# A softmax shift broadcast by two wide matmuls on a table written ahead, in place of four narrow ones

## The reference, cut to what matters

```
h = (x @ W).reshape(N, H, C)
al_s = jnp.einsum('nhc,hc->nh', h, a_src)
al_d = jnp.einsum('nhc,hc->nh', h, a_dst)
e = jax.nn.leaky_relu(al_s[src] + al_d[dst], 0.2)
m = jax.ops.segment_max(e, dst, num_segments=N)
ex = jnp.exp(e - m[dst])
denom = jax.ops.segment_sum(ex, dst, num_segments=N)
alpha = ex / (denom[dst] + 1e-16)
out = jax.ops.segment_sum(h[src] * alpha[:, :, None], dst, num_segments=N)
```

## Time and profile before

| | |
|---|---|
| median of 3 runs | 1179.64 us (1179.39 to 1180.54) |
| the profiled execution's own time | 1182.3 us, of which the span of the trace is 1180.2 us |
| PE busy | 1115.9 us, 95% of the span |
| DVE busy | 839.0 us, 71% |
| ACT busy | 513.9 us, 44% |
| POOL busy | 54.3 us, 5% |
| mean granted clock of TensorE | 0.984 of full speed |

### The profile page before, as it was taken

The page is one execution under the profiler, slowest core; times in us unless marked ns, Lnnn a source line. Parts: engine busy times, 40 slices in busy tenths (PEclk is TensorE's granted clock), DMA queues, the critical chain, the costliest instruction groups (busy, mean ns, idle before and its releaser), DMA issues. The chain is left out here.

```text
span 1180.2 us, 17595 instructions
## 1 busy us (share of the span) xinstructions
PE 1115.9 (95%) x7126; PEld 1045.3 (89%) x7126; DVE 839.0 (71%) x1394; ACT 513.9 (44%) x1052; POOL 54.3 (5%) x50
## 2 busy tenths in 40 slices
PE   5999999999999999999999999858999899999998
PEld 5878886789989998999999999758999899899998
DVE  7998896889768887789668778879757633341163
ACT  4232322376447654556547644335536612431110
POOL 4200001020000000000000000520000000000000
PEclk9999999989999999999999999968999999999999
DMA  6133130021011100201020100022002200000321
GB/s 230 68 103 117 41 122 18 1 63 54 1 42 49 54 1 1 90 22 34 1 68 23 54 1 1 10 91 72 27 27 103 83 1 1 27 14 1 131 77 55
DMA packets 27618, 58.44 MB, mean 50 GB/s; under 512 B 3492, under 2 KB 6152, under 8 KB 27536
## 3 DMA queue, kind: packets, MB, share of 16 engines
q1 hardware_dynamic: 27344, 56.96, 14.5%
q10 hardware_dynamic: 192, 0.32, 0.1%
HBM read 41.73 MB, written 15.54 MB: 49 GB/s over the span
## 5 line engine op out<-in xcount | busy, mean ns | idle before, releaser
L1456 PE MATMUL banks<-hs,ring_hi 128*128 128x258 f32 (+1 forms) x1600 | 299.8, 288 | 6.8 <-DVE z L1051 6.8
L1456 PEld LDWEIGHTS banks<-hs,ring_hi 128*128 128x128 f32 (+1 forms) x1600 | 249.0, 188 | 8.7 <-DVE z L1051 8.0
L1456 PE MATMUL banks<-hs,ring_lo 128*128 128x258 f32 (+1 forms) x800 | 227.1, 284 | 0.0
L247 ACT ACTIVATE e<-banks,al 128x256 f32<-128x256 f32 (+1 forms) x500 | 194.6, 493 | 38.0 <-PE banks L232 38.0
L1456 PEld LDWEIGHTS banks<-hs,ring_lo 128*128 128x128 f32 (+1 forms) x800 | 150.8, 189 | 0.0
L255 ACT ACTIVATE ring_hi<-pf 128x512 fp32r<-128x512 f32 (+1 forms) x125 | 81.6, 652 | 134.7 <-DVE pf L266 130.1
L1486 PE MATMUL banks<-w_hi,oT_hi 128*128 128x384 f32 (+1 forms) x320 | 109.5, 342 | 5.9 <-DVE shiftT L1130 4.5
L1486 PE MATMUL banks<-w_lo,oT_hi 128*128 128x384 f32 (+1 forms) x320 | 108.3, 338 | 0.0
L1486 PE MATMUL banks<-w_hi,oT_lo 128*128 128x384 f32 (+1 forms) x320 | 108.2, 338 | 0.0
L264 DVE TENSOR_TENSOR e<-e 128x512 f32<-128x512 f32 (+1 forms) x125 | 84.5, 676 | 33.2 <-ACT e L247 32.7
L1330 PE MATMUL banks<-w_hi,xT_hi 128*128 128x512 f32 x240 | 96.7, 403 | 1.2 <-DVE xT_lo L827 0.6
(11 more groups left out here) (265 smaller groups left out, 2106.2 us busy)
## 6 DMA issues: line engine op xcount, KB each, us to landing
h_scratch<-stage SPq DMA_DIRECT2D x30, 256.0 KB, 2.0
hs<-h_scratch SPq DMA_DIRECT2D x30, 256.0 KB, 2.9
w_st<-in_L_gnn_W SPq DMA_DIRECT2D x4, 1536.0 KB, 7.4
w_st<-in_L_gnn_W SPq DMA_DIRECT2D x16, 384.0 KB, 3.4
gw_st<-in_L_gnn_W SPq DMA_DIRECT2D x12, 384.0 KB, 4.2
xr<-in_x SPq DMA_DIRECT2D x9, 384.0 KB, 10.1
rows<-in_x SPq DMA_DIRECT2D x9, 384.0 KB, 5.8
x_scratch<-rows SPq DMA_DIRECT2D x9, 384.0 KB
```

What stands on the lines that cost most here:

```text
L247: last = nc.scalar.activation(self.e[:, local % 2, a, i, 0:n], self.p_shift[:, a, 0:n], ACT.Exp, bias=scores[a][:, g * G + i:g * G + i + 1])
L1456: last = nc.tensor.matmul(p_a[0:m, dt, half, 0:HH], wt.ring[a][:, s // G, s % G, dt * P:dt * P + m], hs[:, s, b, half * HH:(half + 1) * HH ...
```

## The change

A new table `spread` (40 partitions, 2 tiles, 128 columns) holds for one chunk the rows of `shiftT` of which all but those of the tile in question are zero: tile dt of the table is the row table times a column of zeros and ones, `own_tile`. With it, one matmul for each part can do both tiles, 256 columns wide; its stationary operand is now the column `of_part` (ones on the rows of that part). So `broadcast` has two matmuls in place of four. The table is written in one of two ways. For chunks 1 to 4 of a head, and 2 to 4 of the second layer, ScalarE writes it (`spread_rows`, two copies with a scale), during the chunk before, behind the exponentials of the third group. For the first chunk of each head, and the first two of the second layer, VectorE writes it from PSUM (`spread_from`, two multiplications), behind the copy into `shiftT`, or in place of it for the very first chunk of the second layer. `own_tile` is made once by GpSimd, `of_part` once by VectorE. `shiftT` has three rows in place of four, used in turn.

```
-        self.shiftT = own("shiftT", [4 * T, HEADS, P], f32r)
+        self.shiftT = own("shiftT", [4 * T, 3, P], f32r)
+        self.spread = own("spread", [4 * T, NDT, P], f32r)
+        self.own_tile = own("own_tile", [4 * T, T], fp32)
+        self.of_part = own("of_part", [4 * T, 2], f32r)
...
-    def broadcast(self, nc, pe, pick, shift_rows, q, c):
+    def broadcast(self, nc, pe, mem, q):
 
         pe.wait_ge(self.e_ready, q * NG + 1)
         for a in range(2):
-            for dt in range(NDT):
-                row = a * T + c * NDT + dt
-                last = nc.tensor.matmul(self.p_shift[:, a, dt * P:(dt + 1) * P],
-                                        pick[:, row:row + 1].to_broadcast([4 * T, P]), shift_rows,
-                                        start=True, stop=True)
+            last = nc.tensor.matmul(self.p_shift[:, a, :], mem.of_part[:, a:a + 1].to_broadcast([4 * T, P]),
+                                    mem.spread[:, :, :].rearrange("r t c -> r (t c)"), start=True, stop=True)
         last.then_inc(self.shift_in, 1)
...
+def spread_from(nc, mem, p_shift, c, done):
+
+    for dt in range(NDT):
+        t = c * NDT + dt
+        last = nc.vector.tensor_scalar(mem.spread[:, dt, :], p_shift, mem.own_tile[:, t:t + 1], None, ALU.mult)
+    last.then_inc(done, 1)
+
+
+def spread_rows(nc, act, mem, slot, c, done):
+
+    for dt in range(NDT):
+        t = c * NDT + dt
+        last = nc.scalar.activation(mem.spread[:, dt, :], mem.shiftT[:, slot, :].bitcast(fp32), ACT.Copy, scale=mem.own_tile[:, t:t + 1])
+    last.then_inc(done, 1)
...
+                        if c + 1 < NC and g == 2:
+                            act.wait_ge(shift_out, h + 1)
+                            spread_rows(nc, act, mem, h % 2, c + 1, spread_done)
...
             def keep_shift(h):
                 dve.wait_ge(shift_t, h + 2)
-                nc.vector.tensor_copy(shiftT[:, h + 1, :], p_g[1][0:4 * T, 0:P]).then_inc(shift_out, 1)
+                nc.vector.tensor_copy(shiftT[:, (h + 1) % 2, :], p_g[1][0:4 * T, 0:P])
+                dve.wait_ge(wt.shift_in, (h + 1) * NC)
+                spread_from(nc, mem, p_g[1][0:4 * T, 0:P], 0, shift_out)
...
-            nc.vector.tensor_copy(shiftT[:, 0, :], p_shift_first).then_inc(shift_out, 1)
+            dve.wait_ge(wt.shift_in, SECOND)
+            spread_from(nc, mem, p_shift_first, 0, shift_out)
...
-            nc.vector.tensor_copy(shiftT[:, 2, :], p_shift_rest).then_inc(shift_out, 1)
+            nc.vector.tensor_copy(shiftT[:, 1, :], p_shift_rest)
+            dve.wait_ge(wt.shift_in, SECOND + 1)
+            spread_from(nc, mem, p_shift_rest, 1, shift_out)
...
                     if s == G - 1 and c + 1 < NC:
-                        wt.broadcast(nc, pe, pick, shiftT[:, h, :], q + 1, c + 1)
+                        pe.wait_ge(spread_done, h * (NC - 1) + c + 1)
+                        wt.broadcast(nc, pe, mem, q + 1)
```

More of the change, by code:

```diff
@@ L383, in first_layer @@
     picked = sem("picked")
+    of_part_ready, spread_done = sem("of_part_ready"), sem("spread_done")
     red_ready = sem("red_ready")
@@ L431, in first_layer @@
     p_shift_first, p_shift_rest = banks[0:4 * T, 6, 2 * P:3 * P], banks[0:4 * T, 6, 3 * P:4 * P]
-    half = second_half(nc, st, mem, *later, tile_in, banks, wt, g_ready, scored)
+    half = second_half(nc, st, mem, *later, tile_in, banks, wt, g_ready, scored, spread_done)
     hs2, hi2_done, lo2_done = half.hs, half.hi_done, half.lo_done
@@ L540, in _ @@
                 pool_.wait_ge(made, 13 + r)
+            nc.gpsimd.tensor_tensor(mem.own_tile[:, :], pick[:, 0:T].bitcast(fp32), pick[:, T:2 * T].bitcast(fp32), ALU.add).then_inc(made, 1)
             nc.gpsimd.iota(codes[:, :, :, :], pattern=[[OFFSET, 2], [0, FIX], [1, WK]], base=0, channel_multiplier=0).then_inc(made, 1)
             nc.gpsimd.iota(place[:, :], pattern=[[1, NCH]], base=0, channel_multiplier=0).then_inc(made, 1)
-            pool_.wait_ge(made, 16)
+            pool_.wait_ge(made, 17)
             for i, (t0, t1) in enumerate(PARTS):
@@ L905, in columns, with part_rows @@
                             attention_column(i, k, a)
+            def part_rows():
+                nc.vector.tensor_reduce(mem.of_part[:, :], pick[:, :].bitcast(fp32).rearrange("r (a t) -> r a t", a=2), AX.X, ALU.max).then_inc(of_part_ready, 1)
             def self_loops():
@@ L942, in _ @@
             edge_keys()
+            part_rows()
             ahead = 0
@@ L1018, in _ @@
             dve.wait_ge(shift_t, 1)
-            nc.vector.tensor_copy(shiftT[:, 0, :], p_s0).then_inc(shift_out, 1)
+            nc.vector.tensor_copy(shiftT[:, 0, :], p_s0)
+            dve.wait_ge(made, 17)
+            spread_from(nc, mem, p_s0, 0, shift_out)
             degree_sums(range(1, 5))
@@ L1405, in spread_first @@
             def spread_first():
+                pe.wait_ge(of_part_ready, 1)
                 pe.wait_ge(shift_out, 1)
-                wt.broadcast(nc, pe, pick, shiftT[:, 0, :], 0, 0)
+                wt.broadcast(nc, pe, mem, 0)
             between = {0: score_columns, 4: turn_top, 5: lambda: turn_shift(0, p_s0), 6: spread_first, 9: degrees}
@@ L1461, in sums @@
                     if s == G - 1 and c + 1 < NC:
-                        wt.broadcast(nc, pe, pick, shiftT[:, h, :], q + 1, c + 1)
+                        pe.wait_ge(spread_done, h * (NC - 1) + c + 1)
+                        wt.broadcast(nc, pe, mem, q + 1)
                     if s == 2 * G - 1 and c == NC - 1 and not final:
                         pe.wait_ge(shift_out, h + 2)
-                        wt.broadcast(nc, pe, pick, shiftT[:, h + 1, :], q + 1, 0)
+                        wt.broadcast(nc, pe, mem, q + 1)
                     if c == NC - 2 and not final:
@@ L1506, in _ @@
             pe.wait_ge(shift_out, HEADS + 1)
-            wt.broadcast(nc, pe, pick, shiftT[:, 0, :], SECOND, 0)
+            wt.broadcast(nc, pe, mem, SECOND)
             def turn_rest():
@@ L1518, in spread_rest @@
                 pe.wait_ge(shift_out, HEADS + 2)
-                wt.broadcast(nc, pe, pick, shiftT[:, 2, :], SECOND + 1, 1)
+                wt.broadcast(nc, pe, mem, SECOND + 1)
             half.tensor(pe, {1: turn_rest, 5: lambda: turn_shift(HEADS + 1, p_shift_rest), 6: spread_rest})
@@ L1544, with second_half @@
     pass
-def second_half(nc, st, mem, x, b2, G1, c1, G2, c2, x2_scratch, out, tile_in, banks, wt, g_ready, scored):
+def second_half(nc, st, mem, x, b2, G1, c1, G2, c2, x2_scratch, out, tile_in, banks, wt, g_ready, scored, spread_done):
     pb, sem = makers(nc, st)
@@ L1719, in scalar @@
                     wt.hi(nc, act, SECOND + c, c, g - 1)
+                if g == 2 and c + 1 < NC:
+                    spread_rows(nc, act, mem, 1, c + 1, spread_done)
             wt.hi(nc, act, SECOND + c, c, NG - 1)
@@ L1865, in vector @@
                 dve.wait_ge(turned, 1)
-                nc.vector.tensor_copy(shiftT[:, 1, :], p_turn).then_inc(turn_out, 1)
+                nc.vector.tensor_copy(shiftT[:, 2, :], p_turn).then_inc(turn_out, 1)
         def row_lo(t):
@@ L1990, in spread_roots @@
                 last = nc.tensor.matmul(p_wide[:, (t - t0) * P:(t - t0 + 1) * P], pick[:, t:t + 1].to_broadcast([4 * T, P]),
-                                        shiftT[:, 1, :], start=True, stop=True)
+                                        shiftT[:, 2, :], start=True, stop=True)
             last.then_inc(wide_ready, 1)
@@ L2027, in tensor @@
                 if s == G - 1 and 1 <= c < NC - 1:
-                    wt.broadcast(nc, pe, pick, shiftT[:, 2, :], SECOND + c + 1, c + 1)
+                    pe.wait_ge(spread_done, HEADS * (NC - 1) + c)
+                    wt.broadcast(nc, pe, mem, SECOND + c + 1)
                 if c == 0 and s in first_chunk:
```

## The result

The changed kernel is slower: 1187.22 us (median of 4 executions) against 1179.72, a ratio of 1.0067, 95% interval 1.0049 to 1.0086, or 7.5 us. Ten executions in all, in two series, give 1187.8. The profiled execution took 1189.7 us, its span 1187.5, mean granted clock 0.983.

What follows compares the result with a forecast made beforehand. TensorE, 95% busy, was taken to bound the kernel. Losses of 5.10 us less gains of 2.83 gave net +2.27 on the median 1179.64, so 1181.9 (chance 0.55); range 1177.0 to 1186.2, the forecast's own 1179.2 to 1185.9.

Steps and rivals of the forecast that it cites:

- Saving of a broadcast: On TensorE, two wide matmuls for four narrow save 0.16 us; 13 count in full, three keep 0.05; all gains 2.83.
- second rival: Narrow matmuls cost less than their place shows: a broadcast saves 0.11 us, net +3.1, 1182.7 us; chance 0.12.
- fourth: Rival: two wide matmuls take as long as four narrow ones; gain 0, net +5.1, 1184.7 us; chance 0.05.
- VectorE behind the copy: Two multiplications behind the copy for the next head, 0.20 us each, lengthen TensorE's wait by 0.40, three times: 1.20 loss.
- ScalarE's pair: Two copies ahead of the fourth group's exponentials, 0.27 us each, delay these by 0.54.
- Chunk 3: In four heads, VectorE 0.54 us late with 0.25 of cover before TensorE's third product: 0.29 lost each, 1.16 in all.
- Chunk 1: In heads 1 to 3, same form as chunk 3, between 0 and 0.29 us; half taken, 3 x 0.145 = 0.44 loss.
- Chunk 0: In heads 1 to 3, VectorE has 0.11 us of slack against 0.54 delay: 0.43 lost, three times, 1.29.
- Head 0: Chunk 0 loses 0, as VectorE waits for GpSimd's clearing; chunk 1 has no cover and loses 0.54 us.
- Second layer: At its chunk 1 TensorE starts 0.94 us later, but at half clock, so 0.47 is lost; later chunks 0.
- third rival: TensorE's clock halves behind the lengthened waits (1.49 to 1.89 us), three heads losing 1.7 each: +5.1 on top, 1187.0; chance 0.10.
- first rival: ScalarE's and VectorE's added instructions fall into time they have anyway; all 25 broadcasts save 0.16: 4.0 us, 1175.6; chance 0.18.

Runs made afterwards that it cites:

- after: The changed kernel as described, against the kernel without the change: 1187.83 us over ten executions, ratio 1.0064.
- before: The kernel without the change, with four narrow matmuls for each broadcast: 1180.45 us over 84 executions in three series, 1179.72 in the first measurement.
- pairs moved: Changed kernel with ScalarE's pairs of copies put behind all five groups' exponentials and, in the first layer, the activation's: 1184.00 us, ratio 1.0028 to the unchanged kernel.
- bank given back at the copy: Changed kernel, but in heads 0 to 2 VectorE's copy frees the bank, its multiplications reading SBUF behind the divisions: 1186.48 us, ratio 1.0049 to the unchanged kernel.
- VectorE's multiplications alone: Unchanged kernel plus VectorE's multiplications behind each copy, the second giving the copy's signal; no ScalarE copies, table unread: 1186.17 us, ratio 1.0052.

## Why the prediction was wrong

The step that failed outright is the clock: the sum put it at nothing, and the rival that had it got a chance of 0.10. The traces show two or three stretches of half clock, 1.5 us each, behind the waits that the change lengthened. The second is the size of ScalarE's losses in chunks 3 and 1, 1.2 us too small. Of the rest it named nearly every place where time was lost, with the right sign.

- **Saving of a broadcast**: 0.16 as forecast, 0.43 from start to next start. What is kept was right too: three of five in a head, and 0.03 to 0.07 in chunk 0 (0.05). The second rival (0.11) and the fourth (none) fall.
- **VectorE behind the copy**: 0.26 for one multiplication, not 0.20; the wait grew by 0.50, not 0.40. Three times 0.10 short. My nearest row was a reciprocal of one column. The Trainium skill ("VectorE: DVE Perf Modes", section "The TRN2 errata — SBUF-src ops pay a fixed extra latency per instruction") has 120 cycles at 0.96 GHz, and the number of columns on top, for an operation of VectorE out of PSUM; by an estimate from it, without a faster mode, 248 cycles or 258 ns. The traces agree, from start to start: 0.258 to 0.259.
- **ScalarE's pair**: 0.585, forecast 0.54. The Trainium skill, in the same section, gives 350 cycles at 1.2 GHz for a ScalarE copy of 128 elements, by an estimate from it 0.292 us. The traces agree: 0.290 to 0.295.
- **Chunk 3**: 0.47 in place of 0.29, four times: 0.72 short. The cover was mis-sized. I let 0.04 us pass from VectorE's end to TensorE's start; after's addition ends at 443.23 and the product starts at 443.38, 0.15. And I had left out that the product behind a wait follows at 0.25 instead of 0.17, 0.08 more.
- **Chunk 1**: 0.31 in place of "half, 0.145", three times: 0.50 short. Having no row for it I halved a term whose form was that of chunk 3. The pair ran into TensorE in full.
- **Chunk 0**: 0.45 against 0.43. **Chunk 2**: 0.05 against 0. **Head 0**: chunk 0 nothing, as forecast (VectorE waits for the clearing either way), chunk 1 0.55 against 0.54, and 0.37 that no view of before could show (the gap above).
- **Second layer**: the delay at chunk 1 was 1.2 against 0.94 (TensorE's wait 4.15 after 2.94); as the half clock behind it ended sooner, 0.53 was left of it in the trace, against my 0.47.
- **The sum**: 0.30 + 0.72 + 0.50 + 0.37 + 0.15 to 0.20 for chunk 2 make 2.1 on top of 2.27, +4.4 at equal clock. The executions say 5.7 ± 0.9, of which about 1 is probably that a stretch in the first layer costs 1.5 and the slope only 1.06.
- **The clock**: the step that failed outright. I forecast a wait of 1.89, just where I had no row, kept 1.49 as "held" and 2.8 as "fell", and gave a fall behind 1.89 only 0.10, though it lay between with nothing to say on which side. The clock fell behind 9 of 12 waits of 1.99 and 2 of 3 of 1.74. My three stretches of 1.7 came to two or three of 1.5 in a profile; with them 4.4 becomes 7.4 to 8.9, measured 7.5. That the third rival's 1187.0 lies 0.2 from the measured time is luck: it had 2.27 of work and 5.1 of clock, the traces about 4.4 and 3.0 to 4.5. Of the signs of being wrong, the one on the granted clock was seen.
- **The first rival** (everything covered, 1175.6) was wrong for this placement. Even with everything moved into idle time the kernel gained 2.8 us on the medians of its series, not 4.0, since the saved time is lost at two of the five places of a head, in that trace too.

What stays open: why the parts do not add up, in time as in stretches. Waits of 1.99 without the longer ones in chunk 0 (pairs moved), waits of 1.80 in chunk 0 without those (bank given back at the copy), and both together bring the mean to 10.5 to 10.6 each time, while VectorE's multiplications alone bring 9.5. The mean counts stretches everywhere in the program, so it does not say how many of them the first layer has; only the profiles do, one for each kernel and two for after. And single steps of TensorE around the waits for the activation differ by up to 0.4 us between the two traces of after, the same kernel.

## What to carry to other kernels

A pair of instructions that costs 0.6 us on an engine with 44% load costs nothing or all of it by where it stands: put it where the timeline shows that engine idle behind it (here 4.3 us on ScalarE, 0.6 on VectorE), and give a bank back at the last read that needs it. A wait of TensorE that grows by half a us must be priced with the clock behind it: here 0.26 us more brought two stretches more, of 1.5 us each in the first layer. Where a term stands between two rows, take a chance near a half for each side, and do not halve a term that has a twin in the trace.

## What the runs showed of the hardware

- Half clock of 3.4 us behind waits of 1.74 to 2.25 us in the middle of dense work, in 12 of 18 cases, and in none of 24 with 1.47 to 1.49 at the same place. Behind waits of 1.78 to 1.81 at another place it came in 2 of 12.
- One operation of VectorE starts 0.45 us behind the one ahead in all eleven traces with three instructions more before it, and 0.08 with none, one or five more.
- GpSimd's clearing of 128x7680 (6.5 us) holds a VectorE operation 128x1280 (bf16 to fp32) up until it is over: that took 2.78, 2.22 and 4.83 us in three kernels, and ended 0.67 to 0.69 behind the clearing in each.
- Two multiplications 40x128 on VectorE have a record of 0.59 us from PSUM and of 0.47 from SBUF.
